# Two-layer grouped linear kernel: the last block product of the first group gets its weight sum from an accumulating DMA instead of a GpSimd add

## What is computed

```python
x: (32, 128, 2048) float32; weight: (2048, 2048); L1 weight: (16, 2048, 2048)
# layer 0: shared weight, bias, and a rank-16 LoRA term chosen per batch
base  = einsum('bsi,oi->bso', x, weight) + bias
low   = einsum('bsi,bri->bsr', x, lora_a[ids7])
delta = einsum('bsr,bor->bso', low, lora_b[ids7])
x = x + base + scale[ids7] * delta
# layer 1: a whole 2048 x 2048 weight chosen per batch
x = x + einsum('bij,bkj->bik', x, weight1[ids14])
```

## Time and profile before

| | us |
|---|---|
| median of 3 runs | 2699.49 |
| lowest, highest | 2697.68, 2699.61 |
| span of the profiled execution | 2696.1 |
| TensorE busy in it | 2684.3 |
| VectorE, ScalarE, GpSimd busy | 1782.7, 1329.9, 730.5 |

### The profile page before, as it was taken

One profiled execution on the slowest core, in us unless ns is written; L12 is line 12 of the kernel. 1 busy time (PEld: TensorE's weight loads), 2 busy tenths in 40 slices (PEclk: granted clock), 3 DMA queues, 4 the chain that ended last, 5 costly groups with the idle time before them and its releaser, 6 DMA issues.

```text
span 2696.1 us, 35567 instructions
## 1 busy us (share of the span) xinstructions
PE 2684.3 (100%) x12826; PEld 2225.0 (83%) x12826; DVE 1782.7 (66%) x1582; ACT 1329.9 (49%) x1398; POOL 730.5 (27%) x586
## 2 busy tenths in 40 slices
PE   8999999999999999999999999999999999999999
PEld 7888888888888888888888888888888888888887
DVE  7758776867455557686745555678674565667865
ACT  3423366666432426666633233566663323456665
POOL 6345611413412111150342111124034111112402
PEclk9999999999999999999999999999999999999999
DMA  8868865677645536668764454889986445489886
GB/s 296 307 233 326 290 203 203 234 272 252 223 152 172 171 110 209 210 233 273 254 207 151 169 179 145 306 309 330 371 333 209 152 157 198 139 304 314 312 322 231
DMA packets 192784, 637.91 MB, mean 237 GB/s; under 512 B 22464, under 2 KB 30816, under 8 KB 192608
## 3 DMA queue, kind: packets, MB, share of 16 engines
q1 hardware_dynamic: 185408, 609.94, 65.6%
q10 hardware_dynamic: 7200, 25.69, 2.4%
HBM read 643.93 MB, written 58.72 MB: 261 GB/s over the span
## 4 chain that ended last, share of the span: by engine, by line
PE 98%; POOL 0%; DMA 0%; DVE 0%; SPq 0%; issue 0%; ACT 0%; POOLq 0%; ACTq 0%
PE acc L971 17%; PE acc L972 17%; PE acc L973 17%; PE acc L918 15%; PE acc L919 15%; PE acc L928 15%; PE acc L874 1%; PE acc L940 1%; POOL raw L584 0%; PE acc L926 0%; DMA raw<-xt 0%; DVE ws L835 0%; DVE ops L835 0%; DMA cb<-xt 0%; DMA cb<-ids 0%
## 5 line engine op out<-in xcount | busy, mean ns | idle before, releaser
L835 DVE TENSOR_TENSOR ws<-raw,ws 128x1024 fp32r<-128x1024 f32 x1020 | 1327.7, 1326 | 432.2 <-ACT ws L710 427.6
L710 ACT CAST ws<-raw 128x1024 fp32r<-128x1024 f32 (+1 forms) x1052 | 1078.5, 1051 | 1047.7 <-PE acc L973 475.9
L971 PE MATMUL acc<-ws,ops 128*128 128x512 f32 (+1 forms) x2048 | 796.9, 389 | 0.0
L972 PE MATMUL acc<-ws,ops 128*128 128x512 f32 (+1 forms) x2048 | 796.9, 389 | 0.0
L973 PE MATMUL acc<-ws,ops 128*128 128x512 f32 (+1 forms) x2048 | 796.8, 389 | 0.0
L918 PE MATMUL acc<-ops,ws 128*128 128x512 f32 x1776 | 693.8, 391 | 0.2
L919 PE MATMUL acc<-ops,ws 128*128 128x512 f32 x1776 | 692.2, 390 | 0.0
L928 PE MATMUL acc<-ops,ws 128*128 128x512 f32 x1776 | 691.4, 389 | 0.0
L616 POOL TENSOR_TENSOR raw<-raw,eye_s 128x128 f32<-128x128 f32 x384 | 350.6, 942 | 1176.8 <-DMA raw<-w 1176.4
L973 PEld LDWEIGHTS acc<-ws,ops 128*128 128x128 f32 x2048 | 384.4, 188 | 80.0
L971 PEld LDWEIGHTS acc<-ws,ops 128*128 128x128 f32 x2048 | 384.4, 188 | 79.5
(11 more groups left out here) (64 smaller groups left out, 583.5 us busy)
## 6 DMA issues: line engine op xcount, KB each, us to landing
raw<-w SPq DMA_DIRECT2D x920, 512.0 KB
raw<-w_sums SPq DMA_DIRECT2D x104, 512.0 KB
raw<-xt SPq DMA_DIRECT2D x96, 512.0 KB
out<-ost SPq DMA_DIRECT2D x128, 256.0 KB, 6.8
cb<-xt SPq DMA_DIRECT2D x60, 512.0 KB, 5.9
w_sums<-raw ACTq DMA_DIRECT2D x32, 512.0 KB, 6.6
ost<-a SPq DMA_DIRECT2D x64, 128.0 KB, 3.0
x_sums<-raw ACTq DMA_DIRECT2D x16, 512.0 KB, 4.3
```

The costliest lines, as they stand in the source:

```text
L710: ins = eng.copy(hi, src)
L835: ins = eng.tensor_tensor(lo, src, hi, ALU.subtract)
L971: eng.matmul(acc, yh, wh, start=begin, stop=False)
L972: eng.matmul(acc, yh, wl, start=False, stop=False)
```

## The change

In the first group, the slices of block product 6 load only their first weight tile through SP. GpSimd then issues a DMA of its own that reads the second weight tile from HBM and adds it onto the first in SBUF, waits until that DMA has landed, and adds the identity. The GpSimd add over two loaded tiles is gone for these eight slices. All other slices, and the later groups, keep their steps.

```diff
                 [("scratch", 1, o), ("w0", o, 1)],
-                [("w0", o + HT, 0), ("w0", o + HT, 1)]][k]
+                [("w0", o + HT, 0)] if not g else [("w0", o + HT, 0), ("w0", o + HT, 1)]][k]
...
-            steps = {1: ["omit", "eye"] if o < KEEP else ["sub"], 4: ["sub"], 5: ["sub"], 6: ["add"]}.get(k, [])
+            steps = {1: ["omit", "eye"] if o < KEEP else ["sub"], 4: ["sub"], 5: ["sub"]}.get(k, [])
...
+        s_second = sem("s_second")
...
                     if not i or n in dadd_no:
                         eng.wait_ge(s_raw[place[r]], landed[r])
+                    if step == "eye" and kind == "W" and index[:2] == (0, 6):
+                        eng.dma_start(t, w0[index[2] + HT, 1], accum_op=ALU.add).then_inc(s_second, 16)
+                        eng.wait_ge(s_second, 16 * (index[2] + 1))
                     if step == "eye":
```

## The result

| | before | after |
|---|---|---|
| median of 3 runs, us | 2699.49 | 2714.27 |
| lowest, highest | 2697.68, 2699.61 | 2713.98, 2715.88 |
| span of the profiled execution | 2696.1 | 2714.1 |

The changed kernel is slower by 0.6%: ratio 1.0059, 95% interval 1.0039 to 1.0079. The forecast was 2715 us. The profiled execution is the longest of the three (2715.88 us).

A forecast was written before the change was run, and what follows sets the result against it. TensorE was taken to bound the kernel, waiting for nobody from block product 0 on. Span 2696.1 plus a stall of 15.5 us gave 2711.6, plus 3.4 to the median about 2715 us; range 2698 to 2735.

The forecast's parts named there:

- The formula: Block product 6: GpSimd's period p is landing plus identity add; TensorE's stall is 8 p - 47.7 us, none up to 5.96.
- I take the median of the nearest row, 7.0 us: Accumulating DMA's landing taken from saves of the same slices, 4.6 / 7.0 / 8.1 us; with 0.9, p = 7.9.
- I let them cancel: DMA landing: SP's thinning loads against the transfer's double read and the colliding save; net zero, 7.0 us kept.
- As good as on time: Slice 0 of block product 6 ready at 291.1 us, due at 290.96; then TensorE waits about 2.2 us before each slice.
- VectorE's evictions stand in the same order and wait for TensorE alone. I add nothing: VectorE's accumulator evictions behind block product 6 were claimed to add no time.
- The clock adds nothing: TensorE's clock, 1.00 in these windows with TensorE still some 70% busy, was claimed to add no time.
- SP and layer 1 not late: SP's later w1 loads and GpSimd's layer-1 identity adds were claimed in time; stall passed on whole, nothing added.
- The prediction's own sign: A shift at the end larger than TensorE's wait in the stretch would prove the passage on what is late next wrong.
- The 3.4 us from span to median: Whole kernel: the median of the runs was taken 3.4 us above the span, turning 2711.6 into 2715 us.
- Hidden: Rival: accumulation lands in under about 5 us, p stays under 5.96, TensorE never waits; 2699.5 us, chance 0.25.
- The double read is paid in full: Rival: DMA engines work through both sources in turn; p = 9.3, stall 26.7 us, 2726 us; chance 0.31.
- The fit of the Trainium skill: GpSimd-issued DMA: 2.0 us fixed plus bytes over 436 GB/s, 3.2 us for 512 KB; p 4.1, no stall; not adopted.

The follow-up runs named there:

- the half rows: Changed kernel with the accumulating DMAs covering only rows 0 to 63 of the 128: 2703.8 us in one run beside 2698.16.
- the last four slices alone: Changed kernel with slices 0 to 3 back to two loads and a GpSimd add; only slices 4 to 7 accumulate, in series: 2702.55 us, ratio 1.0016.
- first slice as before: Changed kernel with slice 0 back to two loads and the GpSimd add; slices 1 to 7 keep the accumulating DMA: 2712.6 us, ratio 1.0049.
- the changed kernel again: The changed kernel rerun without any edit, for its spread between profiles: 2715.24 us beside 2698.16, ratio 1.006.

## Why the prediction was right, and where it was only lucky

- **What bounds the kernel, and where to look:** right. All but 1.15 us of the 18.0 in the profile arises between slice 0 of block product 6 and layer 1, and it is passed on whole (18.0 us at the first and at the last matmul line of layer 1).
- **The formula, eight landings in series against a slice every 5.71 us:** right. In five profiles the span ends 2370.1 to 2370.2 us after the eighth identity add starts; putting two in flight removed three quarters of the loss although each DMA got slower.
- **Its terms:** the predicted start of slice 7 was 330.9 + 15.5 = 346.4, the measured one 348.9. Start of the first DMA 282.8 against 280.8: +2.0, since the input combination ahead of it started at 280.32, not 278.01. First landing 11.7 against 7.0: +4.7. Seven periods 49.5 against 7 x 7.9 = 55.3: -5.8. From the eighth identity add to slice 7, 4.9 against 0.9 + 2.4 = 3.3: +1.6. Together +2.5. So the sum came out well by luck: a first landing sized too low and seven periods sized too high nearly cancel.
- **"I take the median of the nearest row, 7.0 us":** near the 6.6 us measured, but not for a reason that held. The saves themselves fell to 2.7 us in the changed kernel (210 GB/s from 291 to 345 us against 271 before, at a DMA share of 0.79 against 0.74), so they are no measure of the accumulating DMA, which kept its 6.6 us: by the estimate above 5.1 for the read from HBM beside the traffic, 0.6 for GpSimd's path, 0.9 for the accumulation. "I let them cancel" happened to hold.
- **The identity add:** 0.45 us alone, not the 0.9 taken. With the landing this makes the period 7.07.
- **"As good as on time" for slice 0, then 2.2 us before each:** wrong. TensorE waited 5.2 us before slice 0 and then at four places only; the first landing was issued into a stretch with a DMA share of 0.99. That the crowd of SP's loads is what stretched it is argued from this share and from the other first landings of whole tiles (9.2 to 10.9 us); no run emptied the stretch by itself. The crowd alone does not do it: the first plain copy took 7.2 us there from issue to identity add (DMA share 0.93 from 284.25 to 291.4 us), the half rows 8.0 (share 1.01).
- **"VectorE's evictions stand in the same order and wait for TensorE alone. I add nothing":** wrong, and the term that was missed. They stand behind low parts that were now late, which costs 2.1 us at slice 7.
- **The clock adds nothing:** wrong in place and harmless in sum. It was at 1.2 GHz for 5.2 us and cost 2.4 us there, but the matmuls so delayed only took from later waits, since GpSimd's series sets the end: the 2370 us of the table stay the same whether the clock fell for 5.2 us or for less. Where no wait follows that could take it up, as with two in flight or with the last four slices alone, it costs 1.7 us more.
- **SP and layer 1 not late:** right; TensorE has no wait after 348.6 us. The prediction's own sign against this passage, a shift at the end larger than the waits in the stretch, did come: 18.0 against 13.2 us. It does not point at layer 1. Of the 4.8 us between them 2.4 are the clock, 1.15 the late arrival at slice 0, and the rest, 1.2 us, is in the matmuls around the waits.
- **The 3.4 us from span to median:** too much. In the later runs the time of a profiled execution stands 1.8 to 2.2 us above its span, and the profiled execution of before was a short one. In the changed kernel it was the longest of three, so that the median stands only 0.2 us above its span, 3.2 less than assumed. So an error of +2.5 in the span gives a median 0.7 us under the forecast; the nearness of the two medians is luck too.
- **Hidden:** its point was a landing of 5.7 us or less. Plain copies reached 5.7 and half transfers 5.2, and stayed within about 0.2% of before; the real DMA did not. As a rule for what would be hidden it held.
- **The double read is paid in full:** the engines' time did double (about 3 against 1.4 us), but only 0.9 us more showed in the landing of one DMA in flight, and that includes 0.3 us of longer issue. The rule of the Trainium skill ("Collectives: The Full Stack", section "The bandwidth ceiling: the fold count and why AG ≠ RS ≠ AR"), which explains a slow ReduceScatter by the two source reads of its reducing transfers, agrees with the doubled engine time and with 5.1 against 3.6 us per slice when several are in flight; no run here parts the second read from the addition. For one at a time it is not the price that counts.
- **The fit of the Trainium skill** ("DMA: Bandwidth & Descriptors", section "Anatomy of one DMA — SWDGE (gpsimd) path"), 3.2 us as an estimate for this size, is far under both the plain copy (5.7) and the accumulation (6.6) in this traffic. Holding to the row decided the sign.

The kernels with two and three in flight are still 2.5 to 4 us above the kernel before, though their pace of 5.1 us is under 5.71. For two in flight the profile says why: the late first slice and the half clock behind it. The full DMA engines cost nothing there, since no later slice waits. For three in flight the only profile is that of an unusually long execution, so what the usual ones lose stays open, and so does what stretches the first landing.

## What to carry to other kernels

Before a wait for a DMA is put on an engine, multiply: the landing time under the traffic of that stretch, once per tile and in series, against the time in which the consumer uses a tile; here 7.07 against 5.71 us, 1.4 us too much per slice, became 9.5 us over seven slices. If such a DMA must be used, keep two in flight, or put it where a lead has been built up. And look at what stands behind each late instruction in its engine's order, since an eviction that waited there for nothing before becomes a wait of the consumer.

## What the runs showed of the hardware

- An accumulating DMA from HBM onto SBUF, 128 rows of 4 KB in fp32, holds each of the 16 DMA engines for about 3 us, a plain one for about 1.4 us (0.9% and 0.4% of the span for eight). With the engines full, the kernel with it moves 312 GB/s, the one without it 385.
- Issue on GpSimd takes 0.87 us with accumulation and 0.57 without; ScalarE issues the same plain copy in 0.40.
- Half the columns take 0.8 us off a landing of 6.6, half the rows 1.4: by a straight line, an estimate, 3.8 to 5.0 us of the landing time are fixed.
- TensorE's clock was granted at 0.51 for 5.2 us after a wait of 5.18 us, at 0.50 from 309.5 to 315 us after one of 4.56 us (first slice as before), and at 0.65 over the 4.9 us after one of 2.81 us; but it stayed at 1.00 after a wait of 3.58 us in the very same profile as the last (the changed kernel again). With two in flight it was at 0.51 for 3.4 us after a wait of 2.40 us. The length of the single wait alone does not decide.
